# Attention of a gated cross-attention block: context split 122 + 32, the 32 rows stacked, products in three rounded terms

## The reference, cut to what matters

```
Sim    = (hc @ w1) + (hq @ w2) + (hc * w3) @ hq.T + b_sim      # hc: 1024 x 256, hq = ctx: 154 x 256
A      = softmax(Sim, over the 154 context rows)
hq_hat = A @ hq                                                # "attended", 1024 x 256
Batt   = softmax(max over context of Sim, over tokens);  hc_bar = Batt @ hc
feats  = concat[hc, hq_hat, hc * hq_hat, hc * hc_bar]          # 1024 x 1024
out    = feats @ W_qv + b_qv                                   # W_qv: 1024 x 256, four blocks W0..W3
```

## Time and profile before

| | us |
|---|---|
| median of 3 runs | 445.97 |
| the profiled execution's own time | 446.07 |
| its span | 444.2 |
| TensorE busy | 428.3 (96%) |
| VectorE busy | 336.4 (76%) |
| ScalarE busy | 290.0 (65%) |
| GpSimd busy | 116.2 (26%) |
| granted TensorE clock | 1.00 of full speed |

### The profile page before, as it was taken

The page is one execution under the profiler, slowest core; times in us unless marked ns, Lnnn a source line. Parts: engine busy times, 40 slices in busy tenths (PEclk is TensorE's granted clock), DMA queues, the critical chain, the costliest instruction groups (busy, mean ns, idle before and its releaser), DMA issues.

```text
span 444.2 us, 6830 instructions
## 1 busy us (share of the span) xinstructions
PE 428.3 (96%) x2432; PEld 294.7 (66%) x2432; DVE 336.4 (76%) x637; ACT 290.0 (65%) x376; POOL 116.2 (26%) x124
## 2 busy tenths in 40 slices
PE   4799999999999989999999999999999999999997
PEld 3688889988988878444444444444444444888886
DVE  5876669676574676884446799999988888997784
ACT  2577468667646254663443899996587778987750
POOL 1248435576749551100000024333000000000000
PEclk9999999999999999999999999999999999999999
DMA  7950002000200200200000000000000000334442
GB/s 235 327 183 0 1 2 94 2 1 2 94 1 0 96 1 2 94 0 0 0 0 1 0 0 0 1 0 1 0 0 0 0 0 23 120 123 141 142 142 72
DMA packets 20673, 21.14 MB, mean 48 GB/s; under 512 B 825, under 2 KB 20392, under 8 KB 20648
## 3 DMA queue, kind: packets, MB, share of 16 engines
q1 hardware_dynamic: 20628, 20.82, 14.8%
q10 hardware_dynamic: 20, 0.00, 0.0%
HBM read 12.43 MB, written 8.39 MB: 47 GB/s over the span
## 4 chain that ended last, share of the span: by engine, by line
PE 60%; issue 18%; DVE 14%; ACT 6%; DMA 1%; POOL 0%; ACTq 0%; POOLq 0%; DVEq 0%
PE ps L785 12%; PE ps L750 9%; PE ps L566 5%; PE ps L755 5%; PE ps L578 5%; PE ps L584 5%; PE ps L580 5%; DVE cols L1456 4%; PE ps L547 3%; DVE hid L1472 2%; ACT hid L1024 2%; PE ps L556 2%; PE ps L623 1%; PE ps L533 1%; PE ps L615 1%
## 5 line engine op out<-in xcount | busy, mean ns | idle before, releaser
L750 PE MATMUL ps<-xh,wuh 128*128 128x512 f16 x192 | 72.8, 379 | 0.8 <-DVE gq L1495 0.8
L750 PE MATMUL ps<-xh,wul 128*128 128x512 f16 x192 | 72.8, 379 | 0.0
L755 PE MATMUL ps<-xl,wuh 128*128 128x512 f16 x192 | 57.1, 379 | 0.0
L1435 DVE TENSOR_REDUCE cols<-hid x10 | 22.9, 2286 | 24.3 <-ACT hid L1001 24.3
L785 PE MATMUL ps<-wdh,oh 128*128 128x256 f16 x168 | 37.4, 273 | 0.0
L785 PE MATMUL ps<-wdl,oh 128*128 128x256 f16 x168 | 37.4, 273 | 0.0
L484 POOL PARTITION_ALL_REDUCE cols<-cols x4 | 1.5, 365 | 135.0 <-DVE cols L1395 129.2
L1001 ACT ACTIVATE hid<-ps 128x2048 f32 x10 | 18.7, 1875 | 27.5 <-PE ps L755 27.5
L750 PE MATMUL ps<-xh,wgh 128*128 128x512 f16 x96 | 36.4, 379 | 0.0
L750 PE MATMUL ps<-xh,wgl 128*128 128x512 f16 x96 | 36.4, 379 | 0.0
L750 PEld LDWEIGHTS ps<-xh,wuh 128*128 (+1 forms) x192 | 18.8, 98 | 24.1 <-issue 1.8
(11 more groups left out here) (225 smaller groups left out, 1009.7 us busy)
## 6 DMA issues: line engine op xcount, KB each, us to landing
x_scratch<-xa SPq DMA_DIRECT2D x4, 1024.0 KB, 4.4
xo<-x_scratch SPq DMA_DIRECT2D x16, 256.0 KB, 2.7
out_dram<-xo SPq DMA_DIRECT2D x15, 256.0 KB, 2.2
xa<-in_x SPq DMA_DIRECT2D x3, 1024.0 KB, 12.1
xa<-in_x SPq DMA_DIRECT2D x4, 256.0 KB, 4.9
wv<-in_L_xattn_W_qv SPq DMA_DIRECT2D x1, 1024.0 KB, 8.9
wr<-in_L_ffn_w_gate SPq DMA_DIRECT2D x1, 768.0 KB, 10.1
wr<-in_L_ffn_w_up SPq DMA_DIRECT2D x1, 768.0 KB, 11.4
```

The costliest lines, as they stand in the source:

```text
L750: pe.matmul(ps[hf][:, q, :], w_[:, d, ds(k * P, P)], xh[:, d, n], start=d == 0 and w_ is wh, stop=False)
L755: mm = pe.matmul(ps[hf][:, q, :], wh[:, d, ds(k * P, P)], xl[:, d, n], start=False, stop=d == KD - 1)
L1435: dve.tensor_reduce(gmx[:, ds(k * 2 + hf, 1)], unit(hid, k, hf), AX.X, ALU.max, apply_absolute_value=True).then_inc(gm_done, 1)
```

## The change

The context of a batch becomes 122 rows (JM) in one block, and the other 32 (JR) in a second block that is stacked three times (96 rows, JS). Values are split in a high part, rounded to F32R (a 4-byte type of the matmul), and a low part, the difference. For the 122 rows, three products (high x high, high x low, low x high) are three matmuls; for the 32 rows, the stack holds (high, low, high) on one side against (high, high, low) on the other, so that one matmul of 96 rows makes all three. attend so has 8 F32R matmuls of 256 columns in place of 4 fp32 ones. In project, hqT x W1 (A @ ctx) @ W1 becomes A @ (ctx @ W1): context_project makes ctx @ W1 once a batch in fp32 and it is split in the same way, and project_attended uses the split weights directly, with 4 F32R matmuls for each tile in place of two fp32 ones. The copy to hqT is gone; VectorE reads hq_bank itself.

A part of the diff (declarations of tiles and semaphores cut; some semaphores of the same engine are joined, wlink and ulink into link, the l_ ones into bn2_done, mv2_done, vp2_done and rstd2_rdy, without moving an instruction; sc becomes a ring of two):

```diff
...
-JP = J // 2
+JR = 32
+JM = J - JR
+JS = 3 * JR
+RA = 5
...
+            def load_context(b):
+                sp.dma_start(cx[b][0:JM, 0, :], ctx[b, 0:JM, :]).then_inc(cx_in[b], 16)
+                sp.dma_start(cx[b][0:JR, 1, :], ctx[b, JM:J, :]).then_inc(cx_in[b], 16)
+
+            def load_rest(b):
+                for i in range(1, 3):
+                    sp.dma_start(cx[b][i * JR:(i + 1) * JR, 1, :], ctx[b, JM:J, :]).then_inc(cr_in if b == 0 else cx_in[b], 16)
+
             for s in range(NP):
                 sp.dma_start(xa[:, 2 * s:2 * s + 2, :], x_v[:, 2 * s:2 * s + 2, :]).then_inc(x0_in[s], 16)
                 if s == 0:
-                    sp.dma_start(cx[0], ctx_v[0]).then_inc(cx_in[0], 16)
+                    load_context(0)
             sp.dma_start(wv[:], wqv_v).then_inc(wqv_in, 16)
-            sp.dma_start(cx[1], ctx_v[1]).then_inc(cx_in[1], 16)
+            load_rest(0)
+            load_context(1)
+            load_rest(1)
...
-                sp.dma_start(cx[b], ctx_v[b]).then_inc(cx_in[b], 16)
+                load_context(b)
+                load_rest(b)
...
+            def context_low(b):
+
+                pool.wait_ge(ch_rdy, b + 1)
+                pool.tensor_tensor(cl[b][0:JM, 0, :], cx[b][0:JM, 0, :], ch[0:JM, b % 2, 0, :].bitcast(F32), ALU.subtract).then_inc(cl_rdy, 1)
...
+                if s == 2 and b < B:
+                    context_low(b)
...
-                pe.wait_ge(cx_in[b], 16)
-                ge(pe, ngm_rdy, b - 1)
+                pe.wait_ge(cx_in[b], 32 if b == 0 else 64)
                 ge(pe, hc_rdy, b - 2)
-                ge(pe, cbi_rdy, b)
-                for k in range(2):
+                ge(pe, cwl_rdy, b)
+                for k, nk in enumerate((JM, JR)):
                     for d in range(KD):
-                        tr = pe.transpose(m_bank[:, d * J + k * JP:d * J + (k + 1) * JP],
-                                          cx[b][0:JP, k, d * P:(d + 1) * P], ident[0:JP, 0:JP])
+                        at = d * J + k * JM
+                        tr = pe.transpose(m_bank[:, at:at + nk], cx[b][0:nk, k, d * P:(d + 1) * P], ident[0:nk, 0:nk])
                 tr.then_inc(cxT_ps, 1)
+
+            def context_project(b):
+
+                ge(pe, ngm_rdy, b)
+                pe.wait_ge(cbi_rdy, b + 1)
+                pe.wait_ge(cxr_rdy, b + 1)
+                if b == 0:
+                    pe.wait_ge(wqv_in, 16)
+                for d in range(KD):
+                    pe.matmul(m_bank[0:JM, 0:D], cxT[:, d, 0:JM], wv[:, KD + d, :], start=d == 0, stop=d == KD - 1)
+                for d in range(KD):
+                    mm = pe.matmul(m_bank[0:JS, D:2 * D], cxT[:, d, JM:JM + JS], wv[:, KD + d, :], start=d == 0, stop=d == KD - 1)
+                mm.then_inc(cw_ps, 1)
...
-                ge(pe, aT_rdy, n)
-                for k in range(2):
-                    for t in range(2):
-                        tr = pe.transpose(a_bank[0:JP, k * PT + t * P:k * PT + (t + 1) * P],
-                                          sc[:, n % 3, t, k * JP:(k + 1) * JP], ident[:])
+                ge(pe, al_rdy, n)
+                for t in range(2):
+                    pe.transpose(a_bank[0:JM, t * P:(t + 1) * P], sc[:, n % 2, t, 0:JM], ident[:])
+                for t in range(2):
+                    tr = pe.transpose(a_bank[0:JS, PT + t * P:PT + (t + 1) * P], sc[:, n % 2, t, J:J + JS], ident[:])
                 tr.then_inc(at_ps, 1)
 
             def attend(n):
                 b, s, par = place_of(n)
-                pe.wait_ge(aT_rdy, n + 1)
-                ge(pe, hqT_rdy, n)
+                pe.wait_ge(al_rdy, n + 1)
+                pe.wait_ge(cl_rdy, b + 1)
+                pe.wait_ge(cr_rdy, b + 1)
+                ge(pe, pr_rdy, n)
                 for d in range(KD):
-                    for k in range(2):
-                        mm = pe.matmul(hq_bank[:, d * PT:(d + 1) * PT], cx[b][0:JP, k, d * P:(d + 1) * P],
-                                       aT[0:JP, n % 3, k, :], start=k == 0, stop=k == 1)
+                    o_, q = hq_bank[:, d * PT:(d + 1) * PT], slice(d * P, (d + 1) * P)
+                    pe.matmul(o_, ch[0:JM, par, 0, q], ath[0:JM, n % RA, 0, :], start=True, stop=False)
+                    pe.matmul(o_, ch[0:JM, par, 0, q], atl[0:JM, n % RA, :], start=False, stop=False)
+                    pe.matmul(o_, cl[b][0:JM, 0, q], ath[0:JM, n % RA, 0, :], start=False, stop=False)
+                    mm = pe.matmul(o_, ch[0:JS, par, 1, q], ath[0:JS, n % RA, 1, :], start=False, stop=True)
                 mm.then_inc(hq_ps, 1)
+
+            def project_attended(n, t, o_, start):
+
+                q, par = slice(t * P, (t + 1) * P), n // NP % 2
+                pe.matmul(o_, ath[0:JM, n % RA, 0, q], cwh[0:JM, par, 0, :], start=start, stop=False)
+                pe.matmul(o_, ath[0:JM, n % RA, 0, q], cwl[0:JM, par, :], start=False, stop=False)
+                pe.matmul(o_, atl[0:JM, n % RA, q], cwh[0:JM, par, 0, :], start=False, stop=False)
+                mm = pe.matmul(o_, ath[0:JS, n % RA, 1, q], cwh[0:JS, par, 1, :], start=False, stop=False)
+                if t == 1:
+                    mm.then_inc(af_ps, 1)
...
-                    for d in range(KD):
-                        pe.matmul(o_, hqT[:, par, d, q], wv[:, KD + d, :], start=d == 0, stop=False)
+                    project_attended(n, t, o_, True)
...
-                if b == 0:
-                    pe.wait_ge(wqv_in, 16)
+                pe.wait_ge(cwl_rdy, b + 1)
...
+                pe.wait_ge(cwl_rdy, min(b + 2, B))
...
+            for t in range(2):
+                pe.transpose(a_bank[:, PT + t * P:PT + (t + 1) * P], ident[:], ident[:])
...
+                if s == 2 and b < B:
+                    context_project(b)
...
-                    a_ = act.activation(sc[:, n % 3, t, :], sc[:, n % 3, t, :], ACT.Copy, scale=ri[:, c:c + 1])
+                    act.activation(sc[:, n % 2, t, 0:JM], sc[:, n % 2, t, 0:JM], ACT.Copy, scale=ri[:, c:c + 1])
+                    rest = sc[:, n % 2, t, JM:J].unsqueeze(1).broadcast_to([P, 3, JR])
+                    a_ = act.activation(sc[:, n % 2, t, J:J + JS].rearrange("p (c j) -> p c j", c=3), rest, ACT.Copy, scale=ri[:, c:c + 1])
                 a_.then_inc(a_rdy, 1)
 
             def turned_a(n):
                 b, s, par = place_of(n)
                 act.wait_ge(at_ps, n + 1)
-                ge(act, hq_ps, n - 2)
-                act.activation(aT[0:JP, n % 3, :, :],
-                               a_bank[0:JP, :].rearrange("p (k n) -> p k n", k=2), ACT.Copy).then_inc(aT_rdy, 1)
-
-            def attended(n):
-                b, s, par = place_of(n)
-                act.wait_ge(hq_ps, n + 1)
-                ge(act, f_ps, n - 2 * NP + 1)
-                act.activation(hqT[:, par, :, s * PT:(s + 1) * PT], hq_bank.rearrange("p (d n) -> p d n", d=KD),
-                               ACT.Copy).then_inc(hqT_rdy, 1)
+                ge(act, af_ps, n - RA + 1)
+                act.activation(ath[0:JM, n % RA, :, :],
+                               a_bank[0:JM, :].rearrange("p (k n) -> p k n", k=2), ACT.Copy).then_inc(aT_rdy, 1)
+
+            def context_high(b):
+
+                act.wait_ge(cxT_rdy, b + 1)
+                rest = cxT[:, :, JM:J].unsqueeze(2).broadcast_to([P, KD, 2, JR])
+                act.activation(cxT[:, :, J:J + 2 * JR].rearrange("p d (c j) -> p d c j", c=2), rest, ACT.Copy).then_inc(cxr_rdy, 1)
+                act.wait_ge(cx_in[b], 32 if b == 0 else 64)
+                if b == 0:
+                    act.wait_ge(cr_in, 32)
+                ge(act, hq_ps, NP * (b - 1))
+                act.activation(ch[0:JM, b % 2, 0, :], cx[b][0:JM, 0, :], ACT.Copy)
+                act.activation(ch[0:JS, b % 2, 1, :], cx[b][0:JS, 1, :], ACT.Copy).then_inc(ch_rdy, 1)
+
+            def projected_high(b):
+
+                act.wait_ge(cw_ps, b + 1)
+                ge(act, af_ps, NP * (b - 1))
+                act.activation(cwh[0:JM, b % 2, 0, :], m_bank[0:JM, 0:D], ACT.Copy)
+                act.activation(cwh[0:JS, b % 2, 1, :], m_bank[0:JS, D:2 * D], ACT.Copy).then_inc(cwh_rdy, 1)
...
-                ge(act, cbi_ps, b)
-                act.activation(cxT[:], m_bank[:, 0:2 * J].rearrange("p (d j) -> p d j", d=KD), ACT.Copy).then_inc(cxT_rdy, 1)
+                ge(act, cw_ps, b)
+                seen = m_bank[:, 0:2 * J].rearrange("p (d j) -> p d j", d=KD)
+                act.activation(cxT[:, :, 0:J], seen, ACT.Copy).then_inc(cxT_rdy, 1)
...
+                if s == 2 and b < B:
+                    projected_high(b)
...
-                if 3 <= m <= N + 2:
-                    attended(m - 3)
...
+                if s == 0 and b < B:
+                    context_high(b)
...
-                ge(dve, at_ps, n - 2)
+                ge(dve, at_ps, n - 1)
...
-                dve.wait_ge(hqT_rdy, n + 1)
+                dve.wait_ge(hq_ps, n + 1)
                 dve.wait_ge(hT_rdy, n + 1)
```

(29 more changed lines are left out.)

84 lines of the change are left out of this document (42 added, 42 removed).

## The result

The changed kernel takes 453.72 us (median of 4 runs, 452.21 to 454.43) against 445.98 for the one before: a ratio of 1.0172 (95% interval 1.0142 to 1.0201). It is 1.7% slower where I had forecast 434.8 us and given "slower" 9%. The profiled execution took 453.42 us, so 7.35 more than the 446.07 of before.

A forecast was written before the change was run, and what follows sets the result against it. The prediction took TensorE, 96% busy, as the main bound, with VectorE not far behind and other engines pacing some stretches. Start, middle and end summed as 446.07 + 2.0 - 7.2 - 6.1 = 434.8 us, range 428 to 441.5.

The forecast's parts named there:

- The new matmul: In attend and project_attended: an F32R matmul of 256 columns takes 0.109 us, against 0.4325 us for fp32.
- The slow rival of 0.216 us: The 16 F32R matmuls a round: weights not hidden or two cycles a column, 0.216 us each; whole 457 us; 8%.
- my second rival: Middle stretches: VectorE becomes the bound; with 5 us of its idle staying, gain 2.8, start costs 4, whole 441 us; 12%.
- I charge 1.5 us of TensorE idle per four rounds: Middle, 48.01 to 125.29 us: new waits for VectorE before turn_a and turn_context cost 1.5 us per four rounds.
- the 7.2: Middle, 48.01 to 125.29 us: the forecast gain, -(10.2 - 3.0) = -7.2 us, bounds -10.2 and -2.
- the +2.0: Start, 12 to 48 us: batch 0's summary chain begins 2 to 3 us later, partly given back; +2.0 us.
- two to three us late: Start: sign that turn_context(1), waiting for projected_low(0) on VectorE, comes two to three us late.
- I change nothing for it: Whole kernel: clock granted in full (1.00) and TensorE's idle times short, so no allowance for the clock.
- A summary chain over 5 us late: Start: a summary chain over 5 us late was named as a sign that would prove the forecast wrong.
- weights_low(15) goes in, +0.8: 147.97 to 157.15 us, chain to turn_y(11): no saving comes out and weights_low(15) adds 0.8 us.
- my own bounds, +5, -2 and -3: The slow bounds of the three terms: start +5, middle -2, end -3 us.
- the 20.4 us: Whole kernel: net TensorE work removed, -20.4 us, the gain if TensorE set the pace everywhere.

The follow-up runs named there:

- e5: The changed kernel with all split tiles in fp16 in place of F32R, same instructions: 451.53 us, ratio 1.013.
- e2: The changed kernel without weights_low, TensorE reading the rounded weights instead, so the low part is left out of the result: 449.35 us, ratio 1.0077.
- e13: e8 without weights_low on VectorE, so the low part of the attention weights is left out of the result: 443.71 us, ratio 0.9945.
- e14: The changed kernel with the whole context of batch 0 loaded behind all four parts of x: 452.65 us, ratio 1.0142.
- e15: e8 with the whole context of batch 0 loaded behind all four parts of x: 448.73 us, ratio 1.0033.
- e16: e8 with the context of batch 0 loaded behind the second part of x: 447.63 us, ratio 1.0016.
- e8: The changed kernel with the edits of e1, e3, e4 and e7 together: 446.2 us, ratio 0.9996.
- e4: The changed kernel with context_project of batches 0 and 1 in another PSUM bank (y_bank): 450.68 us, ratio 1.0109.
- e6: The changed kernel with attended x W1 back in fp32 and the hqT copy restored, without context_project; attend stays in rounded terms: 455.74 us, ratio 1.0218.
- e7: The changed kernel with summary(3) put behind attended(14) and weights_low(15) on VectorE in round 18: 450.91 us, ratio 1.011.
- e3: The changed kernel with GpSimd's weight_n(1) one round later, from round 18 to 19: 449.2 us, ratio 1.0069.
- e1: The changed kernel with batch 1's x loads issued ahead of the second batch's context: 451.8 us, ratio 1.0117.

## Why the prediction was wrong

**The new matmul: right in kind.** F32R runs at one pass, 0.12 us where I took 0.109. 256 x 0.011 = 2.8 us if TensorE set the pace everywhere, and fp16 at exactly 0.109 changed the whole by 1.9 us (e5). The slow rival of 0.216 us did not happen; its sign was right for other reasons. The middle's cause was in my second rival; the start and the end, which cost most, were in none.

**Middle: "I charge 1.5 us of TensorE idle per four rounds". This step failed.** Forecast for the two stretches: occupied 33.9 + 33.1, idle 3.0, sum 70.1 us. Measured: 35.9 + 34.7 occupied, 5.9 idle, 76.5. Occupied is 3.5 us over the sum; fp16 takes back 1.1 of that. 0.3 is the context's transposes, which I had left as they were because they keep their columns: four took 0.27 us before (80.01 to 80.28) and 0.55 after (85.67 to 86.22). The rest is short gaps, most of them ahead of the waits (the four transposes of turn_y at 81.03 us, ahead of one, count 0.60 us, 0.44 in a stream); no run separates them. But the price is not what decided, since with it gone the windows were as long (e5). VectorE, at 33.09 of 37.53 us, is 88% busy, and I had taken 97% of the floor to leave room. In this ring of engines, each with its queue in order, VectorE did not reach 97%: it kept 4.4 and 5.9 us of idle, on ScalarE's yb and on project_rest. That was my second rival, "If 5 us of it stay, the stretches last 37.8 and 36.7 us"; they lasted 37.5 and 38.9. It had the place and the size right for the first stretch and deserved more than 12%. The second stretch even grew by 0.7 us against the kernel before, and 1.6 us of VectorE's time in it is the meeting of summary(2) with GpSimd. Nor is VectorE alone the bound: without weights_low the middle is 74.7 us (e2, e13), and there TensorE is nearly at its own floor (busy 35.28 of 36.59 us in e2's first four rounds). The two stand some 2 us apart, so no single relief frees the 7.2.

**Start: the +2.0 was mis-sized, it is +8.5.** Its parts: 2.9 us before turn_context(0), from the first loads. I had charged SP's six issues 0.3 us, counting bytes, and asked neither in how many pieces a load of 122 rows lands nor which small load it stands in front of (e14: b_sim at 4.63 or 7.47 us by the context's place alone). No run gave these 2.9 us back; that a late turn_context(0) comes through to rest(0) is seen in e15 and e16, 1.0 and 1.3 us later than e8 there and 2.7 and 2.2 at rest(0). 2.8 us for the wait of turn_context(1) on projected_low(0) and the half clock after it (e4; e6 the same); somewhat over 1 us of it is clock, since e5 with the same wait and the clock at 1.00 had rest(0) at 53.0. That wait I had foreseen, "two to three us late", and then given back to slack in the summary's chain, without asking what a clock that falls would cost: "I change nothing for it", of the clock, was false once there were new idle times. 1.4 us for weights_low (e13 against e8). That is 7.1 of 8.5; the rest was not told apart. "A summary chain over 5 us late" was my own sign of failure, and it came.

**End: "weights_low(15) goes in, +0.8".** It is +4.8. I costed the operation, not its place in VectorE's queue: weights_low(15) stands behind summary(3), which waits for batch_cols(3) (e7), and the summary had moved under GpSimd's weight_n(1), which stretched it from 0.88 to 3.04 us (e3). Behind an idle of 4.96 us attend and project(12) ran at half clock to 164.5 us. The chain I walked was the old one; I had not laid the new summary's time against GpSimd's list.

**Where TensorE is alone the sum held:** -2.3 against -2.6 after turn_y(11), -2.7 against -4.3 before batch_cols(3), the latter less a wait of 0.74 us for ath, the price and short gaps.

The range (428 to 441.5) was narrower than my own bounds, +5, -2 and -3, which add up to 446.1 us. Repaired at four places the change is a draw. So of the 20.4 us that I took off TensorE nothing was left even then: e8's start is still 5.5 us late, and of the middle's 7.2 us 0.8 came out. How the start's 5.5 divide between the first loads and VectorE's added work is not told apart beyond e13's 1.4.

## What to carry to other kernels

An engine at 96% does not mean that a gain on it comes out. Add the new work to the next engine's busy time and compare with the shortened round; here, in rings of queues in order, the second engine set the pace at 85 and 88% busy, so near that count on its pace and not on the difference. For every new wait, look at what stands ahead of its releaser in that engine's queue, and what GpSimd does in that microsecond. Once TensorE gets new idle times, one of 2 us or several of 1.3 to 1.6 us close together, reckon with a stretch at half clock behind them. And look at how many pieces a load of a new shape lands in.

## What the hardware showed that I had not expected

- F32R matmuls of 256 columns with their own 122 x 128 weights start 0.12 us apart, fp16 ones with the same shapes 0.109.
- After idle times of TensorE of 2.15 and 4.96 us the granted clock fell to a mean of 0.57 over 8 us, and to a mean of 0.77 over 14.69 us; F32R starts were then 0.21 us apart. The kernel before, whose idle times were at most 1.6 us after the first 3 us, had 1.00 throughout; e8, with three of 1.33 to 1.55 us within 14 us, fell to 0.57 over 128 to 132 us. In other executions with the same waits the fall was smaller (0.86 over 24 to 36 us in e1) or absent (1.00 in e5), so that single comparisons scatter by 1 to 2 us.
- A VectorE operation of 256 columns with two SBUF inputs took 2.65 us beside a GpSimd operation, 0.48 alone; one of 512 columns with one input in PSUM took 0.68 us beside a GpSimd operation as alone.
- A four-byte load landed between 4.6 and 8.9 us depending on where the loads of the context's rows stood in another queue. The load of 154 rows in 77 partitions landed in 11 pieces by 4.41 us, and with 122 rows in 122 partitions the last four pieces came at 6.83 to 7.06 us.
